# Cross-attention with image tokens on one Trainium2 core: K and Q laid out through DRAM, another prologue, a written-out tail

## The reference

```
q = heads(hidden_states @ W_q);  k_t = heads(text_ehs @ W_k);  v_t = heads(text_ehs @ W_v)
probs_t  = softmax(q k_t^T * attn_scale)
text_out = probs_t v_t
k_ip = heads(ip_ehs @ W_k_ip);  v_ip = heads(ip_ehs @ W_v_ip)
attn_scores = q k_ip^T * attn_scale
qsem = _l2norm(probs_t @ text_ehs)
ip_n = _l2norm(ip_ehs)
sem  = qsem ip_n^T
probs_ip = softmax(attn_scores + SEM_SCALE * sem) * spatial_mask
out = (text_out + probs_ip v_ip) @ W_out + b_out + residual
```

## Time and profile before

| | |
|---|---|
| median of 3 runs | 233.72 us (233.47 to 237.01) |
| the profiled execution | 234.08 us |
| its span, first to last instruction | 232.0 us |
| busy, share of the span: PE / DVE / ACT / POOL | 90% / 82% / 73% / 67% |
| DMA queue, share of 16 engines | 44.6%, 28.38 MB |
| mean granted TensorE clock | 0.958 |

### The profile page before, as it was taken

How to read it: one execution, slowest core, us unless ns; L and a number is a source line. 1 busy time by engine, 2 the same in 40 slices (tenths; PEclk the granted TensorE clock), 3 DMA queues, 4 the chain that set the end, 5 groups by cost and what they waited for, 6 DMA issues and landing times.

```text
span 232.0 us, 6889 instructions
## 1 busy us (share of the span) xinstructions
PE 207.8 (90%) x1562; PEld 192.6 (83%) x1562; DVE 190.8 (82%) x1149; ACT 170.0 (73%) x561; POOL 154.4 (67%) x263
## 2 busy tenths in 40 slices
PE   1948989999999999999999999999999999988433
PEld 1647879998898999999999999999999999977222
DVE  5753778796979798998979897989798979998862
ACT  2063978897978798897969797988888888975000
POOL 5611003649596868788796969696969696979650
PEclk9976999999999999999999999999999999999955
DMA  5405433465355545373736353646454553533030
GB/s 150 124 18 154 104 101 66 124 172 142 104 160 143 149 132 163 87 206 82 204 80 186 104 172 99 167 119 158 132 152 144 145 149 106 143 87 85 1 100 14
DMA packets 46348, 28.57 MB, mean 123 GB/s; under 512 B 7897, under 2 KB 43898, under 8 KB 46330
## 3 DMA queue, kind: packets, MB, share of 16 engines
q1 hardware_dynamic: 46330, 28.38, 44.6%
HBM read 11.11 MB, written 1.52 MB: 54 GB/s over the span
## 4 chain that ended last, share of the span: by engine, by line
PE 61%; DMA 9%; DVE 8%; POOL 7%; ACT 6%; issue 4%; SPq 3%; DVEq 0%; POOLq 0%; ACTq 0%
PE main_ps L746 11%; PE main_ps L748 11%; PE probsT_ps L723 10%; PE pa L686 9%; DMA main_rhs<-g_stage 6%; PE score_ps L706 6%; PE pb L732 5%; POOL rnorm L429 3%; PE pb L758 3%; PE pa L765 2%; ACT probs L497 2%; DVE junk L608 2%; PE pa L775 2%; SPq L324 1%; PE pb L695 1%
## 5 line engine op out<-in xcount | busy, mean ns | idle before, releaser
L497 ACT ACTIVATE probs<-score_ps,negmax 128x124 f32<-128x124 f32 x320 | 93.3, 413 | 0.7 <-DVE negmax L628 0.6
L608 DVE CUSTOM_DVE_ANT_0 junk<-main_ps,probs 128x124 f32<-128x124 f32 x320 | 78.0, 281 | 2.3 <-PE main_ps L748 1.5
L746 PE MATMUL main_ps<-main_rhs,probsT 124*128 124x137 f32 x320 | 65.1, 284 | 1.5 <-DVE small L610 1.4
L748 PE MATMUL main_ps<-main_rhs,probsT 124*128 124x137 f32 x320 | 63.3, 279 | 0.0
L429 POOL TENSOR_TENSOR rnorm<-clamped,exponent 128x20 f32<-128x20 f32 (+1 forms) x16 | 54.8, 3427 | 1.1 <-DVE clamped L556 1.1
L628 DVE TENSOR_REDUCE negmax<-score_ps 128x4 f32<-128x496 f32 x80 | 53.1, 664 | 0.0
L466 ACT ACTIVATE probsT<-probsT_ps 124x512 f32<-124x512 f32 x80 | 51.1, 639 | 2.8 <-PE probsT_ps L723 2.0
L746 PEld LDWEIGHTS main_ps<-main_rhs,probsT 124*128 124x128 f32 x320 | 48.9, 190 | 3.5 <-issue 2.6
L748 PEld LDWEIGHTS main_ps<-main_rhs,probsT 124*128 124x128 f32 x320 | 48.7, 188 | 0.0
L723 PE MATMUL probsT_ps<-ident_sb,probs 128*124 128x128 f32 x320 | 48.2, 273 | 0.0
L723 PEld LDWEIGHTS probsT_ps<-ident_sb,probs 128*124 128x124 f32 x320 | 38.4, 139 | 5.2
(11 more groups left out here) (91 smaller groups left out, 339.2 us busy)
## 6 DMA issues: line engine op xcount, KB each, us to landing
main_rhs<-g_stage SPq DMA_DIRECT2D x16, 660.0 KB, 4.1
vrep<-vip_d SPq DMA_DIRECT2D x16, 320.0 KB, 3.5
k_diag<-k_stack SPq DMA_DIRECT2D x60, 64.0 KB, 2.1
ctxT_sb<-ctxT SPq DMA_DIRECT2D x16, 124.0 KB, 2.6
xT_sb<-xT SPq DMA_DIRECT2D x16, 80.0 KB, 2.0
xn_sb<-xn SPq DMA_DIRECT2D x16, 80.0 KB, 2.0
out<-out_sb SPq DMA_DIRECT2D x16, 80.0 KB, 1.7
k_diag<-k_stack SPq DMA_DIRECT2D x60, 16.0 KB, 2.0
```

Of the source, the lines that this page charges most:

```text
L497: last = act.activation(probs[p][:, h, :], score_ps[(p * G + g) % 2][:, j * TOK:j * TOK + T], ACT.Exp, bias=negmax[p][:, h:h + 1])
L608: dve.tensor_tensor_reduce(junk[:, 2 * r + a, :], u, probs[wb][:, h, :], 1.0, 0.0, ALU.mult, ALU.add, norm2[wb][:, h:h + 1])
L746: pe.matmul(main_ps[r][:, 0:MAIN], probsT[mp][:, 2 * r, :], blk[:, RW - MAIN:RW], start=True, stop=True)
L748: pe.matmul(main_ps[r][:, MAIN:2 * MAIN], probsT[mp][:, 2 * r + 1, :], blk[:, 0:MAIN], start=True, stop=True).then_inc(s_main, 1)
```

## The change

K and Q are now projected transposed: the weights are the stationary side, channels come out on partitions (`project_k`, `project_q`), in two halves of 80. ScalarE rounds the high part of all four halves in one copy, VectorE subtracts for the low part, into `kq_split`; GpSimd's `k_columns` adds the image tokens' K (also projected transposed once in the prologue). SyncE then stores K and Q into DRAM with high and low parts in the repeated order that the stacked layout wants, and loads `k_diag` and `q_stack` from there. `k_stack`, the ten turning matmuls, and `k_split`, `q_split` are gone. The projection of batch b+2 stands at group 4 of window b, its split at group 0 of window b+1, Gram and V at group 1. `g_stage` is one copy, 132 wide. Window -1 is gone; its work is in the prologue, where ScalarE issues the DMAs of W_k, W_q, Q's first stores and load, W_out and the head mask itself. `ip_output` runs on GpSimd in all windows that have it.

The last three batches (13 to 15) do not use `vrep`: their image output is `ip_probs` (80 columns) times one matrix, V_ip spread over the heads (`vspread`) times W_out, made once in the prologue (`vw_sb`) and added to the text part's projection in the same bank. The windows end with 15; what follows is written out per engine.

The diff, cut to its core. Helpers, SyncE and GpSimd, then the splits of ScalarE:

```diff
+        def store_k(eng, n):
+
+            for x in range(2):
+                src = kq_split[:, x, :, :].rearrange("p a t -> p (a t)").bitcast(F32)
+                eng.dma_start(k_d[n, x * CH:(x + 1) * CH, :, :],
+                              src.unsqueeze(1).broadcast_to([CH, 2, 2 * TOK])).then_inc(s_kst, 16)
+
+        def store_q(eng, n):
+
+            for x in range(2):
+                for a in range(2):
+                    eng.dma_start(q_d[n, x * CH:(x + 1) * CH, :, a * S:(a + 1) * S],
+                                  kq_split[:, 2 + x, :, :].bitcast(F32)).then_inc(s_qst, 16)
+
+        def stacked_rows(dram, n, j, rows):
+
+            return bass.AP(dram.tensor, dram.offset + n * G * HG * ROWS * TOK + j * ROWS * TOK,
+                           [[TOK, rows], [HG * ROWS * TOK, G], [1, TOK]])
+
+        def load_k(sp, n):
+            for j in range(HG):
+                sp.dma_start(k_diag[n][ROWS * j:ROWS * (j + 1), :, j, :].bitcast(F32),
+                             stacked_rows(k_d, n, j, ROWS)).then_inc(s_kd[n], 16)
+
+        def load_q(sp, n):
+            sp.dma_start(q_stack[n][:, :, :].bitcast(F32), stacked_rows(q_d, n, 0, HG * ROWS)).then_inc(s_qd[n], 16)
...
+            sp.wait_ge(s_kcol, 1)
+            store_k(sp, 0)
+            sp.dma_start(ctxT_sb[1][:, :, NIP:TOK], ctxT[1]).then_inc(s_ctx_in[1], 16)
+            sp.dma_start(xT_sb[1][:, :, :], xT[1]).then_inc(s_xT_in[1], 16)
+            sp.wait_ge(s_zeros[0], 1)
+            sp.wait_ge(s_kst, 32)
+            load_k(sp, 0)
+            sp.wait_ge(s_gstage, 1)
+            sp.dma_start(main_rhs[0][:, :, D + 1:D + 1 + WIN],
+                         g_stage[:, :].unsqueeze(1).broadcast_to([TOK, NPAIR, WIN])).then_inc(s_grep[0], 16)
+            sp.dma_start(wvip_sb[:, :, :], wvip).then_inc(s_wvip_in, 16)
...
             def window(b, p, i, w):
...
                 if has(w) and has(w, ahead=1):
 
-                    wait(sp, s_kT, b + 1)
-                    wait(sp, s_kq4, b + 1)
-                    sp.dma_start(k_split[T:TOK, :, :, :, :].rearrange("t h c a d -> t (h c a d)").bitcast(F32),
-                                 kip_d[bass.ds((b + 1) * NIP, NIP), :]).then_inc(s_kip_in, 16)
+                    wait(sp, s_kcol, b + 2)
+                    store_k(sp, n)
+                    store_q(sp, n)
                 if has(w) and has(w, ahead=2):
 
-                    wait(sp, s_ctx_mm, b + 1)
-                    sp.dma_start(ctxT_sb[p][:, :, 0:T], ctxT[b + 2]).then_inc(s_ctx_in[p], 16)
-                    wait(sp, s_q_mm, b + 1)
-                    sp.dma_start(xT_sb[p][0:CH, :, :], xT[b + 2]).then_inc(s_xT_in[p], 16)
+                    wait(sp, s_gv_mm, b + 1)
+                    sp.dma_start(ctxT_sb[p][:, :, NIP:TOK], ctxT[b + 2]).then_inc(s_ctx_in[p], 16)
+                    sp.dma_start(xT_sb[p][:, :, :], xT[b + 2]).then_inc(s_xT_in[p], 16)
+                if has(w) and has(w, ahead=1):
+
+                    wait(sp, s_kst, 32 * (b + 2))
+                    load_k(sp, n)
+                    wait(sp, s_qst, 64 * (b + 2))
+                    load_q(sp, n)
                 if has(w, lag=2):
 
+                    if w == 2:
+                        sp.wait_ge(s_vip_out, 16)
                     wait(sp, s_final, b - 3)
                     sp.dma_start(xn_sb[p][:, :], xn[b - 2]).then_inc(s_xn_in[p], 16)
 
-                    wait(sp, s_ipout, 3 * (b - 4) + 1)
-                    sp.dma_start(vrep[p][:, :, :, :].rearrange("s m h d -> s (m h d)"),
-                                 bass.AP(vip_d.tensor, vip_d.offset + (b - 2) * (NIP * C),
-                                         [[0, S], [1, NIP * C]])).then_inc(s_vrep_in[p], 16)
...
-                if has(w, ahead=1):
-
-                    wait(sp, s_scores, G * b)
-                    wait(sp, s_kst03, b + 2)
-                    for j in range(HG if w != -1 else 0):
-                        sp.dma_start(k_diag[n][32 * j:32 * j + 32, 0:G - 1, j, :].bitcast(F32),
-                                     k_stack[32 * j:32 * j + 32, 0:G - 1, :]).then_inc(s_kd03[n], 16)
+                    if w is None or w - 2 < LAST:
+                        wait(sp, s_ipout, 3 * (b - 4) + 1)
+                        sp.dma_start(vrep[p][:, :, :, :].rearrange("s m h d -> s (m h d)"),
+                                     bass.AP(vip_d.tensor, vip_d.offset + (b - 2) * (NIP * C),
+                                             [[0, S], [1, NIP * C]])).then_inc(s_vrep_in[p], 16)
...
+                if has(w) and has(w, ahead=1):
 
                     wait(sp, s_main, NPAIR * b)
                     wait(sp, s_gstage, b + 2)
-                    sp.dma_start(main_rhs[n][:, :, D + 1:D + 1 + NIP + TOK],
-                                 g_stage[:, :].unsqueeze(1).broadcast_to([TOK, NPAIR, NIP + TOK])).then_inc(s_grep[n], 16)
-
-                    wait(sp, s_st4, b + 2)
-                    for j in range(HG if w != -1 else 0):
-                        sp.dma_start(k_diag[n][32 * j:32 * j + 32, G - 1, j, :].bitcast(F32),
-                                     k_stack[32 * j:32 * j + 32, G - 1, :]).then_inc(s_kd4[n], 16)
+                    sp.dma_start(main_rhs[n][:, :, D + 1:D + 1 + WIN],
+                                 g_stage[:, :].unsqueeze(1).broadcast_to([TOK, NPAIR, WIN])).then_inc(s_grep[n], 16)
                 if has(w, lag=3):
 
                     wait(sp, s_final, b - 2)
                     sp.dma_start(out[b - 3], out_sb[n][:, :]).then_inc(s_store[n], 16)
...
+            sp.dma_start(tail_xn[:, :], xn[B - 1]).then_inc(s_tail_xn_in, 16)
+            sp.wait_ge(s_final, LAST)
+            sp.dma_start(xn_sb[0][:, :], xn[B - 2]).then_inc(s_xn_in[0], 16)
+            sp.wait_ge(s_final, LAST + 1)
+            sp.dma_start(out[LAST], out_sb[1][:, :]).then_inc(s_store[1], 16)
+            sp.wait_ge(s_final, LAST + 2)
+            sp.dma_start(out[LAST + 1], out_sb[0][:, :]).then_inc(s_store[0], 16)
+            sp.wait_ge(s_final, LAST + 3)
+            sp.dma_start(out[LAST + 2], tail_out[:, :]).then_inc(s_tail_store, 16)
...
+            def k_columns(b):
+
+                pool.tensor_copy(kq_split[:, 0:2, :, T:TOK].bitcast(F32),
+                                 kip_split[:, :, :, bass.ds(b * NIP, NIP)].bitcast(F32)).then_inc(s_kcol, 1)
+
...
+            pool.wait_ge(s_kip, 1)
+            pool.wait_ge(s_lo, 1)
+            k_columns(0)
...
+            for k in range(TAIL):
+                pool.tensor_tensor(vspread[:, k, :, :].rearrange("p x (h m) -> p x h m", m=NIP),
+                                   vipT_sb[:, :, k, :].unsqueeze(2).broadcast_to([CH, 2, H, NIP]),
+                                   hmask_sb[:, :, :].unsqueeze(3).broadcast_to([CH, 2, H, NIP]),
+                                   ALU.mult).then_inc(s_vspread, 1)
...
+                if has(w) and has(w, ahead=1):
+                    wait(pool, s_lo, b + 3)
+                    k_columns(b + 1)
                 if has(w) and has(w, ahead=2):
-                    wait(pool, s_ctx_mm, b + 1)
-                    pool.tensor_copy(ctxT_sb[p][:, :, T:TOK],
-                                     ipunitT[:, :, bass.ds((b + 2) * NIP, NIP)]).then_inc(s_ipcol, 1)
+                    wait(pool, s_gv_mm, b + 1)
+                    ip_columns(b + 2, p)
...
+            pool.wait_ge(s_rnorm, B - 1)
+            num = bass.AP(small[0], 0, [[NPAIR * SMALL, S], [SMALL, NPAIR], [SMALL - NIP, 2], [1, NIP]])
+            pool.tensor_tensor(fused[:, :, :].rearrange("s (r a) m -> s r a m", a=2), num,
+                               per_head(rnorm, NIP), ALU.mult).then_inc(s_fuse, 1)
+            pool.wait_ge(s_fuse, 2 * (B - 2) + 1)
+            pool.wait_ge(s_ipstage, B - 1)
+            pool.tensor_tensor(fused[:, :, :], fused[:, :, :], ip_stage[:, :, :], ALU.add).then_inc(s_fuse, 1)
+            for k, heads in enumerate((slice(0, HG * PARTED), slice(HG * PARTED, H))):
+                pool.wait_ge(s_tail_stats, 3 * (k + 1))
+                pool.tensor_tensor(tail_rnorm[:, heads], tail_clamped[:, heads], exponent[:, heads],
+                                   ALU.pow).then_inc(s_tail_rnorm, 1)
...
+            act.wait_ge(s_lo, 2)
+            store_q(act, 0)
+            act.wait_ge(s_fill, 2)
+            act.wait_ge(s_gv_mm, 1)
+            gv_stage()
+            v_stages()
+            act.wait_ge(s_qst, 64)
+            load_q(act, 0)
+            act.dma_start(wout_sb[:, :, :], wout).then_inc(s_wout_in, 16)
+            act.dma_start(hmask_sb[:, :, :], hmask).then_inc(s_hmask_in, 16)
...
+                    if g == 0 and has(w) and has(w, ahead=1):
+
+                        wait(act, s_kq_mm, b + 3)
+                        wait(act, s_kst, 32 * (b + 1))
+                        wait(act, s_qst, 64 * (b + 1))
+                        act.activation(kq_split[:, :, 0, :], pb[0:CH, :].rearrange("p (x t) -> p x t", x=4),
+                                       ACT.Copy).then_inc(s_hi, 1)
```

(77 more changed lines are left out.)

653 lines of the change are left out of this document (382 added, 271 removed).

## The result

| | before | after |
|---|---|---|
| median of the runs | 234.26 us (233.47 to 237.01, 4 runs) | 297.3 us (295.82 to 297.67, 4 runs) |
| ratio to before | | 1.269, 95% interval 1.262 to 1.277 |
| span of the profiled execution | 232.0 us | 295.3 us |
| TensorE busy | 207.8 us | 232.7 us |
| mean granted clock over the span | 0.96 | 0.88 |

Single executions of a kernel can be some 1.5% longer than the rest, as the 237.01 us here.

A forecast was written before the change was run, and what follows sets the result against it. TensorE bound the kernel before; after, a ring: SyncE's train 9.13 + `vrep` landing 3.5 + GpSimd 3.8 = 16.4 us. From window 3 at 66.6, eleven turns reach 247.0, end 282.6, plus 2: 284 us, range 250 to 302.

The forecast's parts named there:

- The ring: K columns, SyncE's train, `vrep` landing, next window's `ip_output`, its K columns: 16.4 us a turn, bounds 13.4 to 17.8; chance 0.70.
- `vrep` lands 3.5 us after its issue: Landing term of the ring over `vrep`: 3.5 us, or 4.1 in the upper bound with the Q load in front.
- The start: Prologue: `wvip` issued at 14.5, landing 3.5 later, then TensorE's projection and product; first scores near 25.5, 6 us later.
- The end: Last batch: 14.7 us from first scores to last main matmul, then a 9.6 us tail, 6.6 saved; end 282.6.
- third ring: Over the next context: `ctxT`, `xT` land at +6.7, projection 1.7, splits and copy 3; 11.4 us, taken as covered.
- first ring: The ring through SyncE's train, `vrep` and GpSimd's `ip_output` to the next K columns: 16.4 us a turn.
- second ring: K columns to Q load to scores to K columns: 28.1 us for two windows, 14.1 each; alone binding, chance 0.10.
- Two signs: TensorE's longest wait at the first scores, for `q_stack<-q_d` or `k_diag<-k_d`; TensorE's share falling to near 65%.
- (a): Issue is cheap where one side is DRAM, under 0.32 us: windows 11.85, time 228 us; chance 0.08.
- (b): SyncE's issues cost near 0.35 us: windows about 12.2, time 232 to 235 us; chance 0.04.
- (d): TensorE stays at the low clock for whole windows: 18.2 us each, time 304 us; chance 0.08.
- TensorE's window: TensorE's own work in a steady window falls by 0.2 us, to 11.85 us.

The follow-up runs named there:

- e1: Changed kernel with the loads of `xn` and `vrep` moved to the head of SyncE's window, ahead of its wait for the K columns; 257.2 us.
- e2: Changed kernel with GpSimd's `k_columns` moved ahead of `ip_output`, SyncE's order kept; 253.2 us.
- e5: Changed kernel with four more 0.5 KB loads, into a tile nobody reads, just ahead of `vrep`; 312.4 us.
- e4: Changed kernel with `xn` and `vrep` issued just ahead of the Q load instead of just behind it; 296.7 us.
- e12: Changed kernel, start alone altered: `wvip`, mask, `wout`, head mask loaded first, V_ip times W_out behind the first score matmul; 292.6 us, ratio to before 1.251.
- e8: e10 with TensorE's projection at group 3 instead of 4 and ScalarE's high part at group 4 instead of the next group 0; 235.2 us, ratio to before 1.001.
- e3: Changed kernel with the edits of both e1 and e2; 253.7 us, ratio to before 1.083.
- e10: e3 with the loads of `ctxT` and `xT` also moved to the head of SyncE's window; 254.4 us.
- e11: e9 with the loads of `ctxT` and `xT` issued by ScalarE after its probabilities of group 0, not by SyncE; 229.2 us, ratio to before 0.981.
- e9: e8 with `wvip`, mask, `wout` and head mask loaded first and V_ip times W_out behind the first score matmul; 232.2 us, ratio to before 0.989.

## Why the prediction held, and where it was off

The forecast was 284 us with a range of 250 to 302; 297.3 came. Direction, mechanism and range were right, the size of the loss was 50 us in place of 63.

| term | forecast | measured | rows or run |
|---|---|---|---|
| six stores | 3.66 | 4.05 | 140.59 to 144.64 |
| `ctxT`, `xT` | 1.48 | 1.37 | 144.64 to 146.01 |
| four K loads and the Q load | 3.25 | 2.49 | 146.01 to 148.50 |
| `xn` | 0.64 | 0.62 | 148.50 to 149.12 |
| train with its wake | 9.13 | 8.56 | 140.56 to 149.12 |
| `vrep` lands | 3.5 | 4.5 here, median 4.6 | 149.12 to 153.59 |
| `ip_output` to the end of the copy | 3.8 | 3.8 | 153.59 to 157.38 |
| a turn | 16.4 | 17.2 (mean of eleven) | 70.5 to 259.6 |
| first scores | 25.5 | 27.6 | |
| K columns of window 3 | 66.6 | 70.5 | |
| K columns of window 14 to the last batch's scores | 11.3 | 9.2 | 259.83 to 269.00 |
| from there to the end of the last main matmul | 14.7 | 15.9 | 269.00 to 284.87 |
| the tail behind it | 9.6 | 10.4 | 284.87 to 295.3 |
| span | 282.6 | 295.3 | |

**The ring.** Shown by `e1`, `e2` and `e5`: cut at either place it is gone, lengthened by 1.1 us by its terms it costs 1.2 in each turn. The train was summed 0.6 us too long. The loads from DRAM are issued every 0.45 us and not every 0.65 as the `k_diag` rows of before. The Trainium skill (DMA: Bandwidth & Descriptors, "Issuing engines are not separate DMA queues") says that the time to start a DMA is usually small relative to the DMA itself. For one DMA here that holds loosely (0.45 of 2.1), for fourteen in a row it does not: 8.6 us of issue stand before 4.6 us of landing.

**The step that failed by size** is "`vrep` lands 3.5 us after its issue". The number was that of the kernel before, where the Q load did not exist and the neighbours of `vrep` were loads of 80 KB and less. I had named the Q load in front as a reason for 4.1 and kept it for the bound only. What the runs show is that both neighbours count. With 3.1 us in place of 1.2 to the Q load in front it is 3.8 (`e5`). In `e1`, where it goes out 3.2 us behind `main_rhs` and no large transfer follows it closely, it is 3.6. With the Q load behind it in place of in front it stays 4.7 (`e4`). Eleven turns of the missing 0.8 us (17.2 less 16.4) are 9 of the 13 us by which the time was missed. The rest is the later K columns of window 3, 70.5 for 66.6; the three terms behind the ring miss by 2.1, 1.2 and 0.8 and cancel. By its terms a turn would be 8.56 + 4.6 + 3.8 = 17.0. The mean is higher since single issues now and then take longer: the longest turn, 18.2 us from the copy at 105.00, has 3.62 us for the four Q stores that take 2.54 elsewhere:

```profile
106.52 3.62 SPq L305 DMA_DIRECT2D q_d<-kq_split  x4
```

**The start** was put 2 us too early, and the term is again a landing: `wvip` was issued at 14.42, as summed (14.5), and landed in 5.6 us, not 3.5. TensorE's timeline of the changed kernel:

```profile
20.04 1.25 PE L873 MATMUL main_ps<-ipT_sb,wvip_sb 128*80 128x12 f32 x8 [8.63 <-DMA wvip_sb<-wvip]
...
24.61 3.41 PE L888 MATMUL main_ps<-wout_sb,vspread 80*80 80x160 f32 x12
27.61 1.25 PE L941 MATMUL score_ps<-k_diag,q_stack 128*128 128x512 f32 x2
```

The work behind it took 7.6 us at the low clock, against 7.2 in the sum. `e12` shows that this placement alone costs 4.7 us of the 63.

**The end.** The new tail took 295.3 - 284.87 = 10.4 us behind the last main matmul, forecast 9.6; in `e8` it is 9.6. Against 16.0 before it saves about 6 us, near the 6.6 that were summed.

**The step that was wrong** is the third ring, "even 3 us for the two splits and the copy make 11.4, covered too". It counted durations from SyncE's issue on. It left out where the parts stand in the order of their engines: the low part at the head of VectorE's group 0, the projection at the end of TensorE's group 4. That chain paces at 13.74 us by itself (`e2`, `e3`), about TensorE's 12.24 and the 1.40 it stands for the norms. It lay under the 17.2 of the first ring, so by luck the forecast did not suffer. The second ring, put at 14.1 us a window here and at 13.7 in the expectation for `e1`, was right: `e1` stops at it, and its waits are for the Q load. Since the third ring is as long, the time of `e1` alone does not tell the two apart. `e2` does: its K columns come 3.6 us earlier, by the time that `ip_output` takes (153.59 to 157.19), so its second ring is 27.3 - 3.6 = 23.7 us for two windows, 11.9 each. Its window is 13.74 all the same, and it never waits for the Q load. In `e8` the Q load stands in SyncE's order where `e10` has it, and the window is 12.24.

**Two signs were wrong.** TensorE's longest wait was to be at the first scores; it is at the projection, for `xT` (16.9 us against 10.4 for the Q load). SyncE issues `ctxT` and `xT` behind the six stores, so group 4 of TensorE stands 1.27 us for them at 147.83, before it stands again for the Q load. This wait is in the gap that the ring leaves and costs nothing of its own: 1.0 us of it is left in `e1`, where `ctxT` and `xT` stand behind the same six stores. TensorE's share was put near 65% and is 79%: the forecast left out that its work lasts longer at the lower clock.

**Rivals.** (a) and (b) fell on issue cost: 0.35 us is what `xn` and `vrep` occupy, but the pitch in a row of equal issues in the steady windows was nowhere under 0.44. (d), low clock for whole windows, did not come. The table of windows of the changed kernel over 100 us shows how much of it there was:

```profile
100.00:200.00 100.00, 82.62 (x549) 74.42 (x549) 63.85 (x402) 55.91 (x171) 56.90 (x100) 0.88 0.54 153
```

The columns behind the stretch are its length, the busy time (and count) of TensorE, its weight loads, VectorE, ScalarE and GpSimd, the granted clock, the share of the DMA engines and GB/s. A closer look, at the gap ahead of one window, at the group that follows it and at the next:

```profile
151.50:155.00 3.50, 3.44 (x14) 3.26 (x15) 2.15 (x16) 1.61 (x5) 1.40 (x1) 0.52 0.83 248
155.50:158.00 2.50, 2.50 (x23) 2.41 (x21) 1.98 (x16) 1.92 (x7) 2.22 (x7) 1.00 0.00 0
149.80:151.50 1.70, 0.00 (x0) 0.00 (x0) 0.90 (x4) 0.59 (x1) 0.00 (x0) 1.00 1.01 279
```

Behind the gap the first score group runs at 0.52, close to 1.2 GHz, and the next at 2.4 GHz again. The loss stays inside the gap, as the forecast said. In `e1`, `e2`, `e3`, `e10` and `e8` the clock over 100 to 200 us is 1.00, in `e4` and `e5`, which keep the gap, 0.90 and 0.91.

**TensorE's window** was put at 11.85 us, 12.24 came in `e8` and `e11`. TensorE is busy 99% of it by the profile. The projections did get cheaper: by the starts of one window of `e8` (183.08 to 195.32) K and Q take 1.66 us (1.72 in the sum) and Gram and V 0.89, 2.55 together, where the kernel before spent 3.01 on Gram, V, K, Q and the turns (1.43, 0.43, 0.49, 0.49 and 0.17 by the starts of the window of the earlier trace rows). The 0.46 saved are lost elsewhere. The multiplication by W_out starts 1.22 us behind the transposes of `attn_out`, with a wait for VectorE's copy `oT`, where it was 0.90 before; two lines of `e8`, then two of before:

```profile
190.85 0.38 PE L935 MATMUL pa<-ident_sb,attn_out 128*80 128x128 f32 x2
192.07 0.81 PE L951 MATMUL pa<-wout_sb,oT 81*128 81x160 f32 x4 [0.16 <-DVE oT L740]
135.05 0.38 PE L695 MATMUL pb<-ident_sb,attn_out 128*80 128x128 f32 x2
135.95 0.81 PE L732 MATMUL pb<-wout_sb,oT 96*128 96x160 f32 x4
```

The rest is small steps in the main matmuls of the groups behind the projection. No run moves the transposes, so what holds the window at 12.24 stays open.

**What the change is worth without its rings** follows from the table of starts, `e8` against before: start +8.2, windows -0.3, last batch -0.2, tail -6.3, together +1.3 us, by which the spans differ (without rounding: 8.21, 0.34, 0.23 and 6.34). The shorter tail pays for the later start, and the round trip of K and Q through DRAM buys nothing in the windows. With the start mended and two issues moved off SyncE the tail's gain is left: 229.2 us, 1.9% (1.4 to 2.4) faster than before: clear of no change, not clear of the prediction's 2%.

## What to carry to other kernels

Before work is moved onto an in-order queue, draw the ring: from the event that releases the train, past every DMA that stands ahead of the one that is needed, its landing, and back to that event on the other engine; if the ring is longer than the window of the busiest engine, it is the new window. Then look for the next ring under it, with the places of its parts in the engines' orders and not only with their durations, since cutting the first one brings you just to the second. Price landings with their new neighbours on both sides, and put each DMA whose data is ready early at the head of the queue's window.

## What the runs showed of the hardware that was not expected

- An issue costs SyncE about the same whether it loads 0.5 KB or 80 KB: 0.44 us for the tiny loads (1.77/4), 0.45 for K loads (1.79/4). From the Q load of 320 KB to the next issue it is 0.60. Stores take more, 0.63, be they of 80 or 160 KB (2.54/4 and 1.26/2).
- Landings of the same 320 KB lie between 3.5 and 4.7 us (`vrep`) and between 3.0 and 5.1 us (Q load) by what else is in flight, and by the `vrep` of `e4` a transfer that is issued later slows an earlier one.
- Now and then a single issue takes far longer, at places that differ between kernels. The queue's timeline of `e9` has one K load in the middle of the run:

```profile
91.34 2.06 SPq L315 DMA_DIRECT2D k_diag<-k_d  x1
```

Beside it the transfers of the core nearly stopped for a microsecond (4 and 9 GB/s in the DMA view between 92.5 and 93.7 us, 335 two microseconds later). In `e8` four K loads that took 1.8 to 2.0 us elsewhere took 3.23 at 92.28. The window of `e8` that follows took 14.10 us in place of 12.24. In `e11` an issue of 2.09 us cost its window nothing. No run tells what causes it.
